# A macaron block on one core: the first choices are masked out by POOL instead of VectorE

## What is computed

```python
w, sel = jax.lax.top_k(gate_v, 2)                 # of 8 experts, per row and head
mix_v = einsum('bthk,bthke->bthe', sigmoid(w), one_hot(sel))
v = einsum('bthe,bted->bhtd', mix_v, proj_v)      # values mixed from 8 experts
probs = softmax(q * scale @ k)
attn = einsum('bhij,bhjd->bihd', probs, v)
_, sel_o = jax.lax.top_k(gate_o, 2)
res = einsum('bthe,bthd,efd->bthf', one_hot(sel_o).sum(3), attn, Wo)
x = x + 0.5 * res
```

## Time and profile before

| | us |
|---|---|
| median of 3 runs (lowest, highest) | 2470.3 (2469.51, 2485.37) |
| the profiled execution | 2470.45 |
| its span, first to last instruction | 2468.7 |
| PE busy | 2348.8 |
| ACT busy | 2083.6 |
| DVE busy | 1960.9 |
| POOL busy | 1136.0 |

### The profile page before, as it was taken

How to read it: one execution, slowest core, us unless ns; L and a number is a source line. 1 busy time by engine, 2 the same in 40 slices (tenths; PEclk the granted TensorE clock), 3 DMA queues, 4 the chain that set the end, 5 groups by cost and what they waited for, 6 DMA issues and landing times.

```text
span 2468.7 us, 119467 instructions
## 1 busy us (share of the span) xinstructions
PE 2348.8 (95%) x49920; PEld 2165.5 (88%) x49920; DVE 1960.9 (79%) x3498; ACT 2083.6 (84%) x6373; POOL 1136.0 (46%) x1126
## 2 busy tenths in 40 slices
PE   3999999999999999999999999999999999999997
PEld 3888898989889898888989889899898989989897
DVE  4887877878888788888888788787887887888874
ACT  3988888888888888888888889888888888889896
POOL 3454544535445355354454444553453544544431
PEclk9999999999999999999999999999999999999999
DMA  4565555655656655566656556566665655565564
GB/s 129 160 162 149 150 158 150 160 152 158 170 150 163 163 157 155 156 162 165 158 157 165 149 156 167 165 163 155 169 159 154 170 157 157 157 167 155 160 173 107
DMA packets 519381, 388.09 MB, mean 157 GB/s; under 512 B 214080, under 2 KB 436160, under 8 KB 510656
## 3 DMA queue, kind: packets, MB, share of 16 engines
q1 hardware_dynamic: 518416, 379.60, 57.5%
q10 hardware_dynamic: 432, 0.85, 0.1%
HBM read 191.64 MB, written 188.74 MB: 154 GB/s over the span
## 4 chain that ended last, share of the span: by engine, by line
PE 82%; DVE 8%; ACT 5%; issue 4%; POOL 1%; DMA 1%; SPq 0%; ACTq 0%; DVEq 0%; POOLq 0%
PE psT L453 18%; PE psS L408 15%; PE psT L470 7%; PE psS L496 6%; PE psT L421 6%; PE psT L472 6%; PE psT L471 6%; PE psT L496 5%; PE psT L465 5%; ACT PB L767 4%; PE psT L435 3%; DVE NMAX L647 1%; DVE QK L706 1%; PE psT L502 1%; DVE ST L729 1%
## 5 line engine op out<-in xcount | busy, mean ns | idle before, releaser
L767 ACT ACTIVATE PB<-psS,NMAX 128x256 f32<-128x256 f32 x2048 | 943.5, 488 | 71.3 <-DVE NMAX L647 68.0
L453 PE MATMUL psT<-V,PT 128*64 128x64 f32 x16384 | 550.0, 224 | 42.9 <-issue 42.2
L453 PEld LDWEIGHTS psT<-V,PT 128*64 128x64 f32 x16384 | 508.7, 138 | 74.0 <-issue 48.8
L706 DVE TENSOR_TENSOR QK<-psT,QK 128x512 fp32r<-128x512 f32 x512 | 341.8, 688 | 205.0 <-ACT QK L776 202.6
L408 PE MATMUL psS<-QK 64*128 64x256 f32 x6144 | 480.4, 291 | 0.2
L767 ACT ACTIVATION_READ_ACCUMULATOR PB<-psS,NMAX 128x1 f32 x2048 | 453.3, 221 | 0.0
L408 PEld LDWEIGHTS psS<-QK 64*128 64x128 f32 x6144 | 404.5, 186 | 32.1 <-issue 29.5
L647 DVE TENSOR_REDUCE NMAX<-psS 128x2 f32<-128x512 f32 x512 | 328.6, 683 | 85.7 <-PE psS L408 84.8
L776 ACT ACTIVATE QK<-psT 128x512 fp32r<-128x512 f32 x512 | 298.1, 621 | 112.5 <-PE psT L472 98.1
L875 POOL TENSOR_TENSOR BT<-MT,diagv 128x1024 f32<-128x1024 f32 x128 | 305.9, 2390 | 136.1 <-DMA MT<-MIXd 136.1
L856 ACT ACTIVATE PT<-psS 128x512 f32<-128x512 f32 x512 | 280.1, 604 | 52.2 <-PE psS L496 48.4
(11 more groups left out here) (119 smaller groups left out, 4589.3 us busy)
## 6 DMA issues: line engine op xcount, KB each, us to landing
Vd<-VM SPq DMA_DIRECT2D x128, 512.0 KB, 3.9
V<-Vd SPq DMA_DIRECT2D x128, 512.0 KB, 5.2
AOd<-AO SPq DMA_DIRECT2D x256, 256.0 KB, 3.8
PJd<-PJ SPq DMA_DIRECT2D x64, 512.0 KB, 2.8
PR<-PJd SPq DMA_DIRECT2D x64, 512.0 KB, 4.0
MIXd<-MIX SPq DMA_DIRECT2D x64, 128.0 KB, 1.7
MT<-MIXd SPq DMA_DIRECT2D x64, 128.0 KB, 4.4
MASKd<-MASKR SPq DMA_DIRECT2D x64, 128.0 KB, 4.0
```

What stands on the lines that cost most here:

```text
L453: last = eng.matmul(M[64 * u:64 * u + 64, (t * NT + it) * DH:(t * NT + it + 1) * DH], PT[:, t, jt, cols], V[:, pm % 2, 4 * r + t, jt, :], ...
L706: eng.tensor_tensor(QK[:, 1, ab], bank("qk", m).rearrange("p (k t) -> p k t", k=2), QK[:, 0, ab].bitcast(F32), ALU.subtract).then_inc(free ...
L767: eng.activation(PB[:, ab, j, it, :], psS[:, ab, j, it, :], ACT.Exp, bias=NMAX[:, ab, j, it:it + 1], accum_out=SUM[:, p % 2, it, 4 * r + t ...
```

## The change

DVE's step 6 (GM, one instruction at the end of the second quarter) is taken out. POOL does it in two instructions at the head of its third quarter: FW = F1 * -3e38 in bf16, a handoff through a new semaphore, and GM = FW + GS in f32. DVE's MAXV<-GM, which stood near the head of the third quarter ahead of the copies of AO and OT, now stands behind the XT subtraction and ahead of the two QK subtractions. The program of every other engine is the same.

```diff
+        s_low = semaphore("s_low")
...
-                if r == 2 and runs(q):
-                    eng.wait_ge(s_pick, at + 6)
-                    largest(1, GM[:, :, :])
                 if r == 3 and runs(q):
                     highest(at + 9)
...
                     eng.tensor_tensor(dst[:, 1, :], bank("xturn", p + 3)[:, 0:T], dst[:, 0, :].bitcast(F32), ALU.subtract).then_inc(freed("xturn", p + 3))
+                if r == 2 and runs(q):
+                    eng.wait_ge(s_pick, at + 6)
+                    largest(1, GM[:, :, :])
                 if works(n + 1):
...
-                if r == 1 and runs(q):
-                    eng.wait_ge(s_pick, at + 5)
-                    eng.scalar_tensor_tensor(GM[:, :, :], F1[:, :, :], LOWEST, GS[:, :, :], ALU.mult, ALU.add).then_inc(s_pick)
...
+            def without_first(q):
+
+                eng.wait_ge(s_pick, PICKS * q + 5)
+                eng.tensor_scalar(FW[:, :, :], F1[:, :, :], LOWEST, None, ALU.mult).then_inc(s_low)
+                eng.wait_ge(s_low, q + 1)
+                eng.tensor_tensor(GM[:, :, :], FW[:, :, :], GS[:, :, :], ALU.add).then_inc(s_pick)
...
             for n in QUARTERS:
                 p, r = divmod(n, 4)
+                if r == 2 and runs(p + 2):
+                    without_first(p + 2)
```

## The result

The changed kernel takes 2490.28 us (median of 10 runs, 2484.48 to 2502.02), the kernel before beside it on the same chip 2476.63 us (10 runs, 2469.51 to 2489.82). The ratio is 1.0055, 95% interval 1.0029 to 1.008: half a per cent slower. The profiled execution took 2490.26 us, its span 2488.5.

The account below looks back on a forecast made before the run. TensorE, busy 95%, covers the third quarter; in the fourth, DVE's first NMAX delays the kernel. Terms 0 + 3.9 + 6.0 + 3.3 = 13.2 us on 2470.3 give 2483.5 us, range 2461 to 2512.

Parts of the forecast that it names:

- Removal of GM: End of second quarter into third: taking GM off DVE gains 0 us, covered by TensorE's own work in the third quarter.
- The 0.45 us given back on POOL: POOL's MB pair: without GM beside it, it takes 0.45 us less than 4.32 us.
- The move of MAXV: DVE's third quarter: MAXV, about 0.6 us, behind the XT subtraction fits into idle time; cost 0.
- D: Time of POOL's added step in its third quarter: multiply 0.9, add 1.2, two handoffs 0.2; 2.3 us, ends 2.0 and 4.6.
- Odd passes: Fourth quarters from pass 9 on: BT holds EQ 0.45 us in eight passes, plus 0.3 from another; 3.9 us.
- Even passes: From pass 10 on: BT ends early enough before EQ that POOL's step fits; cost 0 us.
- Passes 3 to 8: Both normalisations on POOL back to back: EQ held 1.5 us in four passes, stalls hiding passes 6 and 8; 6.0 us.
- Start: Before the first scores: EQ 0.95 us later, and the second BT 2.3 us later behind POOL's step; together 3.3 us.
- DVE's busy time: Whole run: a sign of the forecast, down by some 110 us.
- The dear multiply: POOL's multiply nearer XN's row, D 3.5 us, 41 us more: 2511 us; chance 0.22.
- rival 2: Odd passes: the shift tips S<-SV free of POOL's hold, 11 us come back: 2462 us; chance 0.13.

Follow-up runs that it names:

- the kernel with POOL's queue alone: Kernel before, GM and MAXV unchanged on DVE; POOL additionally does the same two operations into tiles nobody reads: 2507.92 us, ratio 1.0111.
- the first experiment: The changed kernel with EQ and its product moved behind the fourth quarter's reduces: 2462.21 us, ratio 0.9928 against the kernel before.

## Why the prediction came out right, point by point

- **Forecast.** 2483.5 us stood against 2490.3, in the direction and by the mechanism named: slower by half a per cent, since POOL's BT comes late and holds EQ. Of the 6.8 us between them 6.3 are the kernel before, 2470.3 as a median of three runs and 2476.6 as one of ten. The difference, 13.2 forecast and 13.65 by the medians, agrees better than its terms do, and that is luck: in the traces the start, passes 3 to 8 and the stall-free odd quarters add up to 3.0 + 10.4 + 6.0 = 19.4 us, the upper end of the interval (7 to 20).
- **Removal of GM: 0.** Right as to TensorE's third quarter (9.57 before and after, and no gain in the kernel without the step). The 0.45 us given back on POOL was in the working, and the kernel with POOL's queue alone shows it.
- **The move of MAXV: 0.** Right (1.0007, 0.9988 to 1.0026).
- **D.** The step that failed in size: "I take 0.9, near the lower row". The multiply takes 1.50 us (2.9 ns an element), so D is 2.7 and not 2.3. The argument from L863, that the per-partition scalars make XN dear, held only half: 512 elements cost less than XN's rate (0.80 us for 128) and more than BT's (2.40 for 1024). The Trainium skill ("GPSIMD Engine Reference", section 3.1) has 769 ns as the best for 512 elements with one input; this multiply, bf16 in and out, measured about twice that.
- **Odd passes: 3.9, most of it 8 x 0.45.** Measured 6.0: seven quarters of 0.75, one of 0.53 and one of 0.20. Two errors partly cancel: D was 0.4 larger, and EQ ends 0.54 us after BT and not its full 0.68. That a stall hides the hold is borne out: in pass 55 the stall is 1.27 us and the quarter 10.20 in both traces, though EQ is held to 1.11 us in the later one. BT ended 0.99 us later in the quarter than before, where 0.55 was forecast.
- **Even passes: 0.** Right; stall-free fourth quarters stay at 9.24 within 0.01.
- **Passes 3 to 8: 6.0.** They cost 10.4, most of it 2.03, 2.00, 1.42, 1.51 and 1.69 in the fourth quarters of passes 3 to 7, and 0.68 in each of the first quarters of 5 and 7, which no term covered. Besides D, three things were left out: a fifth pass pays, TensorE waits for BT itself (0.59 us in pass 4, 1.54 in pass 3), and EQ's product FW can be held as well as EQ (pass 3).
- **Start: 3.3.** Measured 3.04. The shape differs: EQ comes 1.18 us later in the first of the two passes, and the second BT ends at 52.20 instead of 48.56.
- **DVE's busy time** fell by 81.5 and not by some 110 us: EQ and FW<-EQ, now held, took 25 us of it back. The records count the time in which an instruction is held as busy.
- **Rivals.** The dear multiply came a third of the way (D 2.7, between 2.3 and 3.5). Of rival 2, S<-SV coming free, there was no net gain: S or ST was held in 17 passes after, in 18 before. Whether BT meets EQ does hang on when POOL's quarter began, as the last section shows.

The rule of the Trainium skill ("SBUF — State Buffer", section "Who interferes with whom"), that a Vector instruction with two SBUF inputs and a GpSimd instruction that reads SBUF exclude each other for the whole instruction and the earlier one wins, fits the traces in both directions: EQ held up to 2495 ns behind BT, and 681 ns where it began first, BT then taking 2.87 us (pass 3). Against a port shared by bandwidth speaks that BT took 2.40 us beside the held EQ of pass 4, as much as alone (median 2.39).

## What to carry to other kernels

Before moving work to an idle engine, list what stands behind it in that engine's queue and what that will then run beside; 112 us of busy time off DVE were worth nothing that could be measured (0.9985, 0.997 to 1.0), and 2.7 us more ahead of one POOL instruction cost half a per cent. Ask of every instruction that leads a quarter whether it must stand there: putting a 0.68 us compare behind the reduces gave 0.65% (0.9935) with one small edit, more than the change could have brought at best. When a producer is made later, look up every reader of its result on every engine, not only the next step of its own chain; the one missed here cost 4%.

## What had not been expected of the hardware

- POOL's cost per element differs by operation and type: 1.50 us for a bf16 multiply by a constant of 512 elements, 1.17 for a bf16 + f32 add of the same size into f32, 0.80 for 128 elements with two per-partition scalars.
- Holds may propagate. In the profiled change, the seven stall-free odd passes whose fourth quarter took 9.98 are those in which S or ST had been held two to three quarters earlier, at 2.1 to 2.5 us; in the five at 9.24 they had not been. The two between, passes 45 and 53, had the hold too. It is not the only way: in passes 27, 35 and 39, which have stalls, EQ was held (0.82 to 1.11 us) with S and ST free. In pass 25 S was free, MB began 1.75 us ahead of the third quarter instead of 0.89 in pass 17, and BT was through 0.02 us before EQ. One execution shows the pairing; no run here forces it.
- TensorE's idle time inside the value matmuls, 44.8 us in 55 pieces with no releaser, lies in other passes in each kernel's trace: in the fourth quarter of pass 12 it is 1.83 us before, 1.01 after and 0.45 in the first experiment. Each kernel has one trace, so whether it also moves between executions of one kernel, and makes their spread (2451 to 2479 us over ten runs of the first experiment), is not shown. What ends it is open: the trace names none, and no run here isolated it.
